# A two-layer graph network on one core: fewer TensorE signals, one-hots behind the visit scans, and a narrower spacing memset in the first layer

## The chip, the cores and the metric

The kernel runs on 1 core of one Trainium2 chip. The metric is device time in microseconds (us) of one execution, as the median of several runs.

## What is computed

`x` holds 3125 nodes of 128 features. There are 53125 directed edges, sorted by their destination node, each with 32 attributes. Two graph layers with 8 heads of 16 features run one after the other, each on the normalised and rectified nodes, and each adds to `x`:

```python
edge_index = jnp.stack([src, dst])
h = jnp.maximum(_layernorm(x, axis=-1), 0.0)
x = x + _L0_gnn_ref(h, L0_gnn_W, L0_gnn_att, L0_gnn_bias, edge_index)
h = jnp.maximum(_layernorm(x, axis=-1), 0.0)
x = x + _L1_gnn_ref(h, edge_index, edge_attr_32, ...)
# layer 0: e = leaky_relu(a_src[src] + a_dst[dst]); softmax over the edges of a dst; sum of alpha * h[src]
# layer 1: score = q[dst].k[src] / 4 + edge_attr @ We + be; softmax over the edges of a dst;
#          sum of attn * v[src]; projection by Wo; + residual; layernorm with gamma, beta
```

## The kernel before

The edges are cut into tiles of 128, and a "visit" is one tile seen by one block of 125 nodes. Sixteen visits make a group, in four quarters of four visits. There are 28 groups; the last one has two quarters, so each layer has 440 visits. In each layer a loop `run_groups` walks over the groups. It is unrolled, and every engine has its own order of work, written out by hand and joined to the others by semaphores. In step g the loop works on three groups at once: group g is scored (`new`), group q = g-1 goes through the running maxima and the exponentials (`mid`), and group r = g-2 is weighted and summed (`old`). There are 30 steps.

GpSimd (POOL) does one thing in the loop: for each visit it issues an indirect DMA that gathers 128 table rows into `G` (L511), and ahead of each it runs `space(300)`, a memset of 300 int32 on one partition (L497) that nothing reads. `G` is a ring of three groups (UNROLL = 3); before each quarter of group g the gathers wait for `pv_ready` of group g-3, which VectorE gives when it has weighted that quarter (`weigh`, L1405). A row is 136 floats in the first layer and 256 in the second.

In the first layer SyncE loads the ids of each group into `lid_ring` (L385, three groups deep) and, every third group, the attributes of three groups into `attr_in` (L404, L407; one buffer). TensorE spreads ids over the partitions (`spread_ids`, L811), and VectorE turns them into transposed one-hots (`node_rows`, L1215, four of them a group, into `ST`). TensorE expands node terms with them (`expand`, L836); VectorE adds the parts (`part_sum`, L1244), then adds the gathered column of all sixteen visits (`score_sum`, L1266, which waits for the gathers of the whole group), and makes the score (`scores`, L1275). TensorE transposes the scores (L870, L871); VectorE scans them (`edge_scans`, L1301, L1302), keeps the last column (`edge_maxima`, L1309); TensorE collects it (L887, semaphore `hop1`); VectorE scans over the visits (`visit_scans`, L1319, L1321, semaphore `x_done`); TensorE spreads the result back (L899, `hop2`). The sums over a group's edges are matmuls in six batches (`sums(g, u, p)`, L851), added into `acc` by VectorE (`add`, L1432); batches 2 to 5 raise `mm_done`. ScalarE makes the one-hots `S` (L615, L619), the exponentials (L655), and copies.

Beside this the first layer prepares the second one's edge bias: TensorE transposes attributes (L932, semaphore `a_T`), ScalarE copies them into `attrT` (L666, `a_Te`), TensorE multiplies them by `WeBD` one step later (L911, semaphore `a_mm`), and ScalarE copies the product (L660, `a_out`). At the start of step 27 VectorE prepares bias rows (`bias_parts`, L1177 to L1186).

In a full step of the first layer TensorE gives 12 semaphore signals: `t_done` twice, `scoreT`, `hop1`, `hop2`, `a_mm`, four of `mm_done`, `a_T` and `al_mm`. VectorE's order around the change is

```python
edge_scans(); rescale(); edge_maxima()
node_rows(2)
visit_scans()
add(0); add(1); carry(); node_rows(3)
```

## Time and profile before

| what | value |
|---|---|
| three runs | 1488.92, 1489.5, 1489.5 us; median 1489.5 us |
| the profiled execution: its own time | 1486.06 us |
| its span, first to last instruction | 1484.3 us |
| mean granted TensorE clock | 0.668 of full speed |
| busy share of PE, DVE, ACT, POOL | 66%, 63%, 43%, 80% |
| gathers of the first layer, first memset to last issue | 37.28 to 688.32 us |
| gathers of the second layer, likewise | 764.04 to 1420.24 us |

The busy share counts an engine's instructions and not its waits. An engine with the highest share need not be the one that sets the end; for that one looks for the engine that never waits for another, and for who waits for it. All times on the axis of the profile are counted from the span's first instruction.

### The profile page before, as it was taken

How to read it: one execution, taken by the hardware profiler on the slowest of the kernel's cores; microseconds unless marked ns; L12 is line 12 of the kernel's file. 1: busy time of each engine (PE TensorE's matmuls, PEld its weight loads, DVE VectorE, ACT ScalarE, POOL GpSimd, SP SyncE). 2: the span in 40 equal slices, each digit the busy share in tenths (PEclk: the TensorE clock that was granted, in tenths of full speed). 3: DMA queues.
4: the chain of work that ended last, by engine and by line, in shares of the span. 5: the costliest groups of instructions: out<-in, count | busy, mean ns of one | idle time of the engine just before them, and what ended most of it. 6: DMA issues, size and time to landing. Idle time of an engine off the chain costs nothing.

```text
span 1484.3 us, 21963 instructions
## 1 busy us (share of the span) xinstructions
PE 980.2 (66%) x4985; PEld 817.4 (55%) x4985; DVE 929.5 (63%) x3002; ACT 636.9 (43%) x1699; POOL 1190.4 (80%) x1806
## 2 busy tenths in 40 slices
PE   5547557777667776676575766676676856566674
PEld 4335446656555565564355655666565746455564
DVE  6446556665665666567834666666666666666578
ACT  5624343453434434341367343444445344444404
POOL 5888888888888888884048888888888888888820
PEclk9655555555555555555686778786867688787765
DMA  6332222222223222222133333333333233333311
GB/s 141 72 69 47 71 49 53 63 71 48 70 48 70 48 69 48 63 48 75 57 112 93 89 88 90 86 89 89 90 89 88 87 89 89 89 89 87 89 29 44
DMA packets 54209, 110.41 MB, mean 74 GB/s; under 512 B 16876, under 2 KB 30848, under 8 KB 53956
## 3 DMA queue, kind: packets, MB, share of 16 engines
q0 software_dynamic: 36288, 91.12, 23.5%
q1 hardware_dynamic: 16483, 17.39, 4.3%
q8 instruction: 46, 0.75, 0.2%
q14 instruction: 79, 0.65, 0.1%
q10 hardware_dynamic: 1313, 0.50, 0.1%
HBM read 100.60 MB, written 8.81 MB: 74 GB/s over the span
## 4 chain that ended last, share of the span: by engine, by line
POOL 39%; issue 6%; DVE 5%; PE 3%; ACT 1%; DMA 0%; DVEq 0%; POOLq 0%; SPq 0%; ACTq 0%
POOL G L511 29%; POOL pad_i L497 10%; PE bank L851 2%; DVE halves L1074 1%; DVE acc L1432 1%; DVE PV L1405 0%; DVE mv L1081 0%; DVE G L1572 0%; DVE hn L1580 0%; DVE xs L1526 0%; DVE hn L1525 0%; DVE hn L1524 0%; PE bank L899 0%; DVE G L1569 0%; DVE hn L1523 0%
## 5 line engine op out<-in xcount | busy, mean ns | idle before, releaser
L511 POOL DMA_INDIRECT G<-table,idx_all x880 | 870.6, 989 | 143.2 <-issue 124.0
L851 PE MATMUL bank<-PV,S 128*125 128x144 f32 x1760 | 446.0, 413 | 135.8 <-DVE PV L1405 74.8
L851 PEld LDWEIGHTS bank<-PV,S 128*125 128x125 f32 x1760 | 369.5, 284 | 164.1 <-issue 121.4
L1432 DVE TENSOR_TENSOR acc<-acc,bank 125x144 f32 x880 | 259.5, 295 | 235.1 <-PE bank L851 154.8
L497 POOL MEMSET pad_i<- 1x300 int32 x880 | 297.1, 338 | 18.8 <-DMA table<-h0b 9.8
L615 ACT ACTIVATE S<-iota_n,lid 128x125 f32<-128x125 f32 x880 | 275.8, 387 | 0.5 <-DVE pen L1169 0.5
L834 PE MATMUL bank<-qe,ST 125*128 x880 | 144.5, 316 | 40.1 <-DVE prod L1225 22.7
L1405 DVE TENSOR_TENSOR PV<-G,PV 128x512 f32<-128x512 f32 x220 | 150.2, 684 | 19.6 <-issue 19.4
L619 ACT ACTIVATE S<-S,ones 128x500 f32<-128x500 f32 x220 | 156.6, 712 | 7.2
L628 ACT ACTIVATE ST<-bank 125x512 f32<-125x512 f32 x110 | 62.6, 596 | 218.7 <-PE bank L899 119.1
L834 PEld LDWEIGHTS bank<-qe,ST 125*128 125x128 f32 x880 | 126.2, 221 | 50.5 <-issue 49.5
L820 PE MATMUL bank<-ident,S 128*125 128x128 f32 x440 | 91.4, 344 | 61.1 <-ACT S L619 50.3
L1225 DVE TENSOR_TENSOR prod<-bank,G 128x512 f32<-128x512 f32 x110 | 74.8, 680 | 87.8 <-DMA G<-table,idx_all 66.9
L820 PEld LDWEIGHTS bank<-ident,S 128*125 128x125 f32 x440 | 79.7, 250 | 67.4 <-ACT S L619 55.6
L655 ACT ACTIVATE EP<-DD 128x256 f32<-128x256 f32 (+1 forms) x56 | 20.2, 360 | 166.6 <-DVE DD L1369 130.8
L1215 DVE TENSOR_SCALAR ST<-bank,vcol 125x512 bf16<-125x512 f32 x110 | 81.5, 743 | 16.2 <-PE bank L811 9.5
L870 PE MATMUL bank<-ident,es 128*128 128x128 f32 x28 | 12.2, 435 | 104.7 <-DVE sc L1275 96.3
L1234 DVE TENSOR_REDUCE raw<-prod 128x32 f32<-128x512 f32 x110 | 74.3, 675 | 1.1
L670 ACT ACTIVATE AL<-bank 125x8 f32<-125x8 f32 x56 | 9.9, 177 | 149.2 <-PE bank L944 125.9
L1266 DVE TENSOR_TENSOR raw<-es,G 128x128 f32<-128x128 f32 x28 | 8.4, 300 | 101.6 <-DMA G<-table,idx_all 99.3
L870 PEld LDWEIGHTS bank<-ident,es 128*128 128x128 f32 x28 | 4.9, 173 | 120.9 <-DVE sc L1275 110.8
L871 PE MATMUL bank<-ident,sc 128*128 128x128 f32 x56 | 23.1, 412 | 68.8 <-DVE sc L1278 64.6
(220 smaller groups left out, 1257.9 us busy)
## 6 DMA issues: line engine op xcount, KB each, us to landing
G<-table,idx_all POOLq DMA_INDIRECT x880
prod<-in_edge_attr_dram SPq DMA_DIRECT2D x8, 672.0 KB
table<-G SPq DMA_DIRECT2D x12, 224.0 KB
bias_rows<-qe SPq DMA_DIRECT2D x1, 1664.0 KB, 5.8
table<-h0b SPq DMA_DIRECT2D x8, 178.5 KB
out_dram<-G SPq DMA_DIRECT2D x8, 168.0 KB
prod<-in_edge_attr_dram SPq DMA_DIRECT2D x8, 90.0 KB
xs<-in_x_dram SPq DMA_DIRECT2D x1, 504.0 KB
```

Of the source, the lines that this page charges most:

```text
L497: pool.memset(pad_flat[0:1, 0:width], 0).then_inc(s_space, 1)
L511: pool.indirect_dma_start(G[:, u, v, 0:w], None, table, bass.IndirectOffsetOnAxis(ap=idx_all[:, g * GV + v:g * GV + v + 1], axis=0)).then_ ...
L615: last = act.activation(S[:, u, v, :], iota_n[:, 0:BN], ACT.Abs, bias=lid[:, bass.ds(g * GV + v, 1)], scale=-1.0)
L619: act.activation(S[:, u, QV * j:QV * j + QV, :], S[:, u, QV * j:QV * j + QV, :], ACT.Relu, bias=ones[:, 0:1], scale=-1.0).then_inc(s.sem[" ...
L820: last = pe.transpose(tp[j % 2][0:BN, k * P:k * P + P], S[:, u, QV * j + k, :], ident[:, :])
L834: last = pe.matmul(ex[j % 2][:, k * F:k * F + F], ST[:, v, :], nodes[:, bass.ds(off, F)], start=True, stop=True)
L851: last = pe.matmul(sums_bank(p)[0:BN, at:at + H * SLOT], S[:, ur, v, :], PV[:, v, :, :].rearrange("p h k -> p (h k)"), start=True, stop=True)
L1215: ve.tensor_scalar(ST_b[:, QV * j:QV * j + QV, :], tp[j % 2][0:BN, :].rearrange("p (v e) -> p v e", v=QV), node, None, op0=ALU.is_equal).t ...
L1225: ve.tensor_tensor(prod[:, j % 2, :].rearrange("p (v f) -> p v f", v=QV), ex[j % 2][:, :].rearrange("p (v f) -> p v f", v=QV), G[:, u, QV ...
L1234: ve.tensor_reduce(raw[:, QV * j:QV * j + QV, :].rearrange("p v h -> p (v h)"), prod[:, j % 2, :].rearrange("p (c d) -> p c d", d=DH), AX. ...
L1405: ve.tensor_tensor(PV[:, QV * j:QV * j + QV, :, 0:DH], rows, PV[:, QV * j:QV * j + QV, :, DH:DH + 1].to_broadcast([P, QV, H, DH]), ALU.mul ...
L1432: ve.tensor_tensor(a, a, o, ALU.add).then_inc(s.sem["acc_added"], 1)
```

## The change

It has three parts, all in the first layer.

1. TensorE gives 9 signals in a full step in place of 12. `t_done` comes after the second `spread_ids` of a group alone (for group 0 also after the fourth); `a_mm` is given for the first group alone, `a_T` for the first two. Who waited for them now waits for a later signal of TensorE that stands behind the same work: the one-hots of the last two quarters and the id loads for `hop1`, the product's readers for batch 2 of the sums (`wait_attr_product`), the transposes' readers for batch 4 (`wait_attr_T`). For that the transposes of the attributes go ahead of batch 4 of the sums in TensorE's order.
2. On VectorE `node_rows(2)` comes behind `visit_scans()`.
3. The spacing memset has 280 columns in the first layer; in the second it keeps 300.

```diff
+        def wait_attr_product(eng, q):
+            if q > 0:
+                wait(eng, L[0]["mm_done"], sums_done(q - 1, 2))
+            else:
+                wait(eng, a_mm, q + 1)
+        def wait_attr_T(eng, g):
+            if g > 1:
+                wait(eng, L[0]["mm_done"], sums_done(g - 2, 4))
+            else:
+                wait(eng, a_T, g + 1)
...
             def load_ids(g, u):
-                wait(sp, L[0]["t_done"], transposed(0, g - UNROLL, 3))
+                wait(sp, L[0]["hop1"], g - UNROLL if g > UNROLL else 0)
+                wait(sp, L[0]["t_done"], 2 if g == UNROLL else 0)
...
-                wait(sp, a_T, g)
+                wait_attr_T(sp, g - 1)
...
-                            space(300)
+                            space(300 if n else 280)
...
-                        wait(act, a_mm, q + 1)
+                        wait_attr_product(act, q)
...
-                            wait(act, a_T, g + 1)
-                            wait(act, a_mm, g)
+                            wait_attr_T(act, g)
+                            wait_attr_product(act, g - 1)
...
-                    if j % 2:
+                    if j == 1 or (j == 3 and g == 0):
                         last.then_inc(s.sem["t_done"], 1)
...
-                        last.then_inc(a_mm, 1)
+                        if q == 0:
+                            last.then_inc(a_mm, 1)
...
-                    if 3 * old > 8:
-                        sums(g, u, 4)
                     if n == 0 and has_attr(g, new):
                         pe.wait_ge(s_attr, 48 * (i + 1))
                         wait(pe, a_Te, g)
                         for k in range(QV):
                             last = pe.transpose(tp[0][:, k * P:k * P + P], attr_in[:, u, k * P:k * P + P], ident[:, :])
-                        last.then_inc(a_T, 1)
+                        if g < 2:
+                            last.then_inc(a_T, 1)
+                    if 3 * old > 8:
+                        sums(g, u, 4)
...
-                wait(ve, a_mm, AG)
+                wait_attr_product(ve, AG - 1)
...
-                        wait(ve, s["t_done"], transposed(0, g, j))
+                        if j < 2 or g == 0:
+                            wait(ve, s["t_done"], g + 1 + (g > 0 or j > 1))
+                        else:
+                            wait(ve, s["hop1"], g)
...
                     edge_maxima()
+                    visit_scans()
                     node_rows(2)
-                    visit_scans()
```

## Rows read from the trace of the kernel before

**Rows 1.** The profile's page: POOL's busy time, and the chain's shares by engine.

```profile
PE 980.2 (66%) x4985; PEld 817.4 (55%) x4985; DVE 929.5 (63%) x3002; ACT 636.9 (43%) x1699; POOL 1190.4 (80%) x1806
...
POOL 39%; issue 6%; DVE 5%; PE 3%; ACT 1%; DMA 0%; DVEq 0%; POOLq 0%; SPq 0%; ACTq 0%
```

**Rows 2.** Waits of POOL, first layer (us in total, times, longest us).

```profile
POOL G L511 <- issue: 63.7, 391, 0.4
POOL pad_i L497 <- DMA table<-h0b: 9.8, 1, 9.8
```

**Rows 3.** Windows of the gathers (L511) alone: first layer, second layer.

```profile
37.28:688.32 651.04, 432.58 (x440) 0.57 0.26 61
...
764.04:1420.24 656.20, 438.05 (x440) 0.75 0.31 89
```

**Rows 4.** Windows of the memsets (L497) alone: first layer.

```profile
37.28:688.32 651.04, 148.56 (x440) 0.57 0.26 61
```

**Rows 5.** Waits of DVE, 76 to 680 us.

```profile
DVE raw L1266 <- DMA G<-table,idx_all: 87.2, 17, 11.5
DVE acc L1432 <- PE bank L851: 83.5, 42, 4.0
DVE acc L1432 <- remote: 26.6, 14, 6.4
```

**Rows 6.** Timeline of POOL, end of group 26 (start us, us, engine, line).

```profile
675.24 0.34 POOL L497 MEMSET pad_i<- 1x300 int32 x1
675.74 0.95 POOL L511 DMA_INDIRECT G<-table,idx_all  x1 [0.16 <-POOL pad_i L497]
```

**Rows 7.** Timeline of DVE, step 26 and what follows.

```profile
673.43 0.55 DVE L1244 TENSOR_REDUCE es<-bank 128x128 f32<-128x384 f32 x1
678.59 0.37 DVE L1266 TENSOR_TENSOR raw<-es,G 128x128 f32<-128x128 f32 x1 [4.61 <-DMA G<-table,idx_all]
...
679.90 0.17 DVE L1177 MEMSET prod<- 96x128 uint32 x1
```

**Rows 8.** Timeline of DVE, steps 27 and 28.

```profile
696.11 0.28 DVE L1266 TENSOR_TENSOR raw<-es,G 128x128 f32<-128x128 f32 x1
...
701.23 0.23 DVE L1319 TENSOR_TENSOR_SCAN D<-rows,D,bank 8x16 f32<-8x16 f32 x1 [0.37 <-PE bank L887]
```

**Rows 9.** Groups by shape: memsets of POOL (busy us, mean ns).

```profile
L497 POOL MEMSET pad_i<- 1x300 int32 x880 | 297.1, 338 | 18.8 <-DMA table<-h0b 9.8 <-DMA table<-G 9.0
...
L453 POOL MEMSET ST<- 112x896 f32 x1 | 0.8, 836 | 0.0
...
L444 POOL MEMSET S<- 8x512 int32 x1 | 0.5, 519 | 0.3 <-POOLq L1607 0.3
...
L447 POOL MEMSET pad_i<- 1x130 int32 x1 | 0.2, 196 | 0.0
```

**Rows 10.** Timeline of POOL between the layers: gathers with no memset between.

```profile
709.33 0.93 POOL L523 DMA_INDIRECT G<-bias_rows,tidx  x1 [0.30 <-issue]
710.56 0.93 POOL L523 DMA_INDIRECT G<-bias_rows,tidx  x1 [0.30 <-issue]
```

**Rows 11.** Timeline of DVE, step 15 around the moved one-hot.

```profile
401.58 0.18 DVE L1309 TENSOR_TENSOR RH<-Vsel,FR 128x32 f32<-128x32 f32 x1
402.31 0.75 DVE L1215 TENSOR_SCALAR ST<-bank,vcol 125x512 bf16<-125x512 f32 x1 [0.55 <-PE bank L811]
402.97 0.23 DVE L1319 TENSOR_TENSOR_SCAN D<-rows,D,bank 8x16 f32<-8x16 f32 x1
```

**Rows 12.** Timeline of PE, the same step.

```profile
402.20 0.28 PE L887 MATMUL bank<-RH,Hsel 128*8 128x32 f32 x2
...
411.61 1.77 PE L851 MATMUL bank<-PV,S 128*125 128x144 f32 x6 [1.16 <-issue]
413.18 1.06 PE L932 MATMUL bank<-ident,prod 128*128 128x128 f32 x4
```

**Rows 13.** Timeline of SyncE's queue: the attributes of groups 15 to 17.

```profile
389.70 0.79 SPq L404 DMA_DIRECT2D prod<-in_edge_attr_dram  x2
```

**Rows 14.** Timeline of POOL and of DVE at one long gather.

```profile
550.94 1.63 POOL L511 DMA_INDIRECT G<-table,idx_all  x1 [0.16 <-POOL pad_i L497]
...
550.87 0.27 DVE L1374 TENSOR_SCALAR OHF<-iota_n,first_lid 8x125 f32<-8x125 f32 x1
```

**Rows 15.** Waits of PE, 76 to 680 us.

```profile
PE bank L870 <- DVE sc L1275: 87.6, 20, 10.8
```

More of the change, by code:

```diff
@@ L266, in gnn_kernel @@
         NODE_SEMS = ("halves", "xc", "std", "inverse", "scales", "hn", "hT_ps", "hT", "feat", "feat_out", "feat_done")
-        LOOP_SEMS = dict(S_ready=QUARTERS, distances=QUARTERS, t_done=2 * GROUPS - 1, st_ready=QUARTERS, expanded=8, qk_done=0,
+        LOOP_SEMS = dict(S_ready=QUARTERS, distances=QUARTERS, t_done=GROUPS + 1, st_ready=QUARTERS, expanded=8, qk_done=0,
                          score_parts=GROUPS, scores_ready=GROUPS, es_ready=GROUPS, scoreT=GROUPS, esT_ready=GROUPS,
```

## The prediction

> **What bounds the kernel now.** I read the page first. GpSimd has the highest busy share, 80%, and the chain that ended last is 39% GpSimd [rows 1]. The chain is drawn back only to 685 us, so its share speaks of the second layer, and the first has to be read from its waits. GpSimd's waits come next. In the first layer's 651.04 us [rows 3] it waits for another engine once, 9.8 us at the start for the table's write; all else is 0.16 us or so between the end of a memset and the gather behind it [rows 2]. It never waits for the ring of three groups. So the stretch is 440 times one period: 651.04 / 440 = 1.480 us, made of a memset of 148.56 / 440 = 0.338 us [rows 4], a gather of 432.58 / 440 = 0.983 us [rows 3], and 0.16 us between them [rows 6]. A group of sixteen takes 23.7 us.
>
> Who waits for GpSimd? VectorE at L1266 stood idle for the gathers 17 times between 76 and 680 us, 87.2 us in all [rows 5], and TensorE behind it 87.6 us for the scores [rows 15]. The last time is in step 26: the last gather of group 26 ends at 675.74 + 0.95 = 676.69 [rows 6], its rows are used at 678.59, 1.9 us later, and VectorE had been idle for 4.61 us [rows 7]. From there the gathers matter no more. Group 27 has only 8 of them, issued by 688.32, and L1266 of that group runs at 696.11 with no wait [rows 8]. So the first layer ends by this path: 432 periods of GpSimd, 1.9 us to land, then steps 26 to 29 at VectorE's and TensorE's own pace (`bias_parts` from 679.90 [rows 7], 696.11 and so on).
>
> **The memset, 300 to 280 columns.** The trace has no memset of 280. Between 130 and 300 columns the time rises from 196 to 338 ns [rows 9], 0.835 ns a column; between 300 and 512 from 338 to 519, 0.854; between 512 and 896 from 519 to 836, 0.826. Twenty columns are 16.5 to 17.1 ns. I take 16.8 ns, near the middle and from the two slopes that meet at 300. On the path lie 432 memsets: 432 x 0.0168 = 7.3 us (bounds 7.1 and 7.4). Does the gather start sooner by as much? From one gather's end to the next's start are now 0.34 + 0.16 = 0.50 us. Gathers with no memset between them follow at 0.30 us and are no longer, 0.93 us [rows 10]. The gap has 0.20 us of room over that, and 0.017 us is far inside it. The lower bound of this term, if the gap grew back in full, would be nothing.
>
> **What gathers cost beside DVE.** A gather is mostly 0.95 us; 440 of them at that would be 418 us, and they took 432.58 [rows 3], so 14.6 us is excess of single long ones. The one at 550.94 took 1.63 us, and on VectorE L1374 (a tensor_scalar from SBUF to SBUF) was running as it began [rows 14]. Such hits hang on where in VectorE's step a gather begins, and a shorter memset shifts that by up to 16 x 0.017 = 0.27 us over a group. The second layer, same memset, has 438.05 / 440 = 0.996 us, 12.4 ns more a gather [rows 3]. If the first layer came to that, 432 x 12.4 ns = 5.4 us would be given back; if it lost as much excess as that, it would gain 5.4 more. I take no change, since VectorE's step stays tied to the gathers by L1266, with 2 us either way. The Trainium skill says why, in its page SBUF — State Buffer, section Who interferes with whom: VectorE in a two-port mode, which a tensor_scalar may enter, and GpSimd lock each other out of a shared pair of ports for a whole instruction. The row at 550.94 agrees with it, and by it the shorter memset would neither add nor remove a hit as such: the sum stays.
>
> **The signals and their new waits.** Three signals fewer on TensorE remove no instruction, only the signal on one. The trace shows no price for a signal alone; below it is nothing, and above it is what TensorE's time could give if it were on the path. It isn't: in the loop VectorE, and TensorE with it, wait for gathers, by 4.61 us in step 26. So I cost it at nothing, in this stretch by that cover. The Trainium skill's page TensorE: Matmul & The Clock Gate, section The cost: per-tile semaphore tail, has 26.3 ns for each signal that ends a matmul; by that three signals in 26 steps would be an estimate of 2.1 us of TensorE's time, and if it lay on the path the sum would be 9.4 us. No row shows it.
>
> The waits that come later: ScalarE's L660 now waits for batch 2 of the sums, and L666 for batch 4 in place of the transposes. Transposes (1.06 us) and batch 4 (1.77 us) change places [rows 12], so that pair ends when it ended. TensorE was even idle for 1.16 us ahead of batch 4, and the transposes need nothing from VectorE, so they go into that gap: up to 1 us of TensorE gained a step, hidden too. Behind batch 4, VectorE's `add(11)` waits, and behind that the step's end; both move inside the cover. SyncE: the attributes of groups 15 to 17 were issued at 389.70 [rows 13] and first used at 413.18, 23.5 us later; the wait comes at most one batch later, 1.77 us. The ids are loaded two steps ahead of their use, and `hop1` comes 0.28 us of matmul behind the last `spread_ids`. Behind these two SyncE's queue holds only the next such loads. Nothing there.
>
> **The one-hot behind the scans.** Now VectorE, done with L1309 at 401.76, idles 0.55 us for the ids, runs the one-hot and finds `hop1` done [rows 11]. After the change it must first wait for L887, which ended at 402.48 [rows 12]: 0.72 us idle in place of 0.55. That is 0.2 us a step; the tail's 0.37 [rows 8], where no one-hot stands there already, is the other reading. The one-hot itself comes some 0.5 us later, and `expand(g, 2)`, `part_sum` and the rest of the score wait for it. All of it has 4.61 us of cover in step 26; without that cover 26 x 0.2 = 5.2 us (9.6 us at 0.37). With the period shorter by 16 x 0.0168 = 0.27 us a group, about 4 us of cover are left. What is late next is still the gathers.
>
> **The tail and the rest.** Step 27 has two quarters, no attributes and no `node_rows(2)`; steps 28 and 29 have no new group. So from 678.59 on the same instructions run, and `bias_parts` waits for batch 2 of step 26 where it waited for the product just ahead of it; VectorE came to it at 679.90 with both long done. The stretch between the layers and the second layer are unchanged: they start 7.3 us sooner. The second layer is tied to its own gathers, 656.20 us [rows 3].
>
> **Sum.** -7.3 us, with nothing for the rest. Against the profiled execution that is 1486.06 - 7.3 = 1478.8 us (its span 1484.3 to 1477.0; 1.8 us lie around the span). The median of the runs is 3.4 us above the profiled execution's time, and I take the difference as it is: 1489.5 - 7.3 = 1482.2 us. 0.2% of the kernel is 3.0 us, which is about what a measurement can tell from no change.
>
> **The rivals.**
> - Collisions eat the gain: gathers get as long on average as in the second layer, 0.996 us. For it: excess varies, and the phase shifts. Against: VectorE's phase follows the gathers. 7.3 - 5.4 = 1.9 us gained, 1487.6 us.
> - Slower by the same hits at full strength: each group has one gather hit as at 550.94, 1.63 - 0.95 = 0.68 us. 27 groups x 0.68 = 18.4 us of excess, on top of the smaller hits the trace now has, against 14.6 now. It decides from the point where a mean gather grows by more than 16.8 ns, so to 1.000 us in the first layer. If all the larger hits came on top of today's excess, it would be +18.4 - 7.3 = 11 us, 1500.6 us. Against: among 440 gathers that have every phase already, most miss. The skill's rule of the lock speaks for the mechanism, not for the number.
> - The loop stops being bound by gathers, because the one-hot's wait and later signals cost more than 4 us a step. Then the first layer grows by the excess over 4 us, 26 times. At 0.2 to 0.4 us of cost it doesn't come to that; what does occur now and then is a long wait of VectorE for TensorE, up to 6.4 us [rows 5]. One of these in step 26 would make L1266 late by 6.4 - 4.3 = 2.1 us: 5.2 us gained, 1484.3 us.
> - The memset doesn't shorten the period (the gap grows back): 1489.5 us. Against it [rows 10].
> - More than forecast: hits get rarer (all of 5.4 us: 12.7 us gained, 1476.8 us), or TensorE's signals count after all (9.4 us, 1480.1 us).
>
> **How the numbers follow.** The forecast, a gain of 5 to 9.5 us with 7.3 as its middle, gets 0.72. It holds the small stall in step 26 and 2 us of hits either way: 1480 to 1484.5 us. More than that gets 0.08. Hits that leave 1 to 3 us get 0.08, no shorter period 0.05, slower by hits 0.05, slower by a loop bound elsewhere 0.02. Faster by over 0.2%: 0.72 + 0.08 = 0.80. Within: 0.13. Slower: 0.07. The range goes from 1478.5 (part of the "more" case) to 1486.0 us (half of the gain of the forecast lost), and leaves about 2 in 10 outside.
>
> **What would show it.** L497 of the first layer at about 321 ns and of the second at 338. The first layer's gathers from 37.3 to about 680.9 us (440 x 16.8 ns = 7.4 sooner), GpSimd with no wait for VectorE. L1266 of group 26 at about 671.3, still waiting for the gathers, by some 4 us. L1319 in mid-layer with a wait of some 0.7 us for L887, and the one-hot with none. L932 ahead of the third last L851 of a step. Between L1266 of group 26 and the end of the span the same 805.7 us as now (1484.3 - 678.59). The prediction is wrong if gathers of the first layer have a mean over 0.99 us, if GpSimd shows waits for L1405, or if L1266 of group 26 no longer waits for them.

## The result and the profile after

| | before | after |
|---|---|---|
| median of 20 runs each, same chip | 1489.5 us (1487.08 to 1491.88) | 1491.41 us (1489.35 to 1494.64) |
| span of the profiled execution | 1484.3 us | 1487.6 us |
| mean granted TensorE clock | 0.668 | 0.687 |

The ratio is 1.0016, with a 95% interval from 1.0009 to 1.0023. The forecast of 1482.2 us was wrong in sign, and its range, 1478.5 to 1486.0 us, doesn't hold the time.

The memset did what was forecast. The windows of the changed kernel's first layer, gathers (L526) in the first line and memsets (L512) in the second (stretch, its length, busy us and count, clock, DMA share, GB/s):

```profile
37.20:693.45 656.25, 444.85 (x440) 0.59 0.25 61
37.20:693.45 656.25, 141.68 (x440) 0.59 0.25 61
```

The memsets take 141.68 / 440 = 322 ns, 16 ns less than in [rows 4], and 6.9 us less in all. The gathers take 444.85 us where they took 432.58 [rows 3]: 1.011 us each, 12.3 us more in all. 12.3 - 6.9 = 5.4 us, and the stretch has grown by 5.2 us, from 651.04 to 656.25. What follows it, from L1286 of group 26 to the end, was 1.9 us shorter (803.8 us against 805.7), so the span grew by 3.3 us. The question of the case is the length of the gathers.

Who waits is as it was, only more so. The changed kernel's waits of POOL, 37 to 694 us, and of DVE, 76 to 690 us (total, times, longest):

```profile
POOL G L526 <- issue: 55.5, 342, 0.4
POOL G L526 <- POOL pad_i L512: 15.8, 98, 0.2
POOL pad_i L512 <- DMA table<-h0b: 9.2, 1, 9.2
...
DVE raw L1286 <- DMA G<-table,idx_all: 162.9, 26, 11.3
DVE acc L1452 <- PE bank L866: 42.1, 30, 1.6
DVE D L1339 <- PE bank L902: 18.5, 25, 0.8
```

GpSimd never waits for VectorE. VectorE waits for gathers in every step, 162.9 us in place of 87.2, and its long waits for TensorE and for "remote" are gone [rows 5]. The wait for `hop1` that the new order makes is there, 18.5 / 25 = 0.74 us a step, and hidden.

Now one full step. The timeline of the changed kernel, POOL and DVE, from 428 to 436 us (start, duration):

```profile
428.71 0.67 DVE L1425 TENSOR_TENSOR PV<-G,PV 128x512 f32<-128x512 f32 x1
428.99 1.23 POOL L526 DMA_INDIRECT G<-table,idx_all  x1 [0.16 <-POOL pad_i L512]
...
432.13 0.95 POOL L526 DMA_INDIRECT G<-table,idx_all  x1 [0.16 <-issue]
433.46 0.27 DVE L1394 TENSOR_SCALAR OHF<-iota_n,first_lid 8x125 f32<-8x125 f32 x1
433.56 1.59 POOL L526 DMA_INDIRECT G<-table,idx_all  x1 [0.16 <-issue]
433.65 0.67 DVE L1425 TENSOR_TENSOR PV<-G,PV 128x512 f32<-128x512 f32 x1
434.47 0.13 DVE L1400 TENSOR_SCALAR DF<-DF 8x1 f32<-8x1 f32 x1
434.96 0.21 DVE L1407 TENSOR_SCALAR R<-ident,DF 8x8 f32<-8x8 f32 x1
```

Two gathers are long here, and a weighting runs in each: `weigh(2)`, of the third quarter, in the first and `weigh(3)` in the second (both L1425). The first weighting ends at 429.38, the gather 0.84 us later, at 430.22; the second ends at 434.32, the gather 0.83 us later. At first I read that the second gather ends with L1407 (435.17), and blamed the streak of small tensor-scalar instructions; the last experiments are about that.

### The profile page after: what moved, and what is told of

It is laid out like the page before. It is cut to its first block, busy times and chain, and to the rows that moved or that the text cites. A ratio compares the mean times of both kernels' runs of the same rounds, so it can differ in the third digit from the quotient of the medians.

```text
span 1487.6 us, 21963 instructions
## 1 busy us (share of the span) xinstructions
PE 919.6 (62%) x4985; PEld 765.0 (51%) x4985; DVE 928.3 (62%) x3002; ACT 637.0 (43%) x1699; POOL 1195.3 (80%) x1806
## 4 chain that ended last, share of the span: by engine, by line
POOL 39%; issue 6%; DVE 5%; PE 3%; ACT 1%; DMA 0%; DVEq 0%; POOLq 0%; SPq 0%; ACTq 0%
POOL G L526 29%; POOL pad_i L512 10%; PE bank L866 2%; DVE halves L1091 1%; DVE acc L1452 1%; DVE PV L1425 0%; DVE mv L1098 0%; DVE G L1592 0%; DVE hn L1600 0%; DVE xs L1546 0%; DVE hn L1545 0%; DVE hn L1544 0%; ACT hn L580 0%; DVE G L1589 0%; DVE hn L1543 0%
## 5 line engine op out<-in xcount | busy, mean ns | idle before, releaser
L526 POOL DMA_INDIRECT G<-table,idx_all x880 | 881.8, 1002 | 142.7 <-issue 110.8
L866 PE MATMUL bank<-PV,S 128*125 128x144 f32 x1760 | 420.3, 395 | 96.6 <-DVE PV L1425 84.0
L866 PEld LDWEIGHTS bank<-PV,S 128*125 128x125 f32 x1760 | 352.1, 271 | 123.6 <-issue 113.8
L1452 DVE TENSOR_TENSOR acc<-acc,bank 125x144 f32 x880 | 259.1, 294 | 122.5 <-PE bank L866 86.4
L512 POOL MEMSET pad_i<- 1x280 int32 (+1 forms) x880 | 290.6, 330 | 17.9 <-DMA table<-h0b 9.2
L1425 DVE TENSOR_TENSOR PV<-G,PV 128x512 f32<-128x512 f32 x220 | 150.3, 684 | 19.3 <-issue 19.2
L849 PE MATMUL bank<-qe,ST 125*128 x880 | 129.6, 293 | 32.4 <-DVE prod L1245 32.2
L849 PEld LDWEIGHTS bank<-qe,ST 125*128 125x128 f32 x880 | 112.5, 200 | 43.1 <-issue 42.3
L1286 DVE TENSOR_TENSOR raw<-es,G 128x128 f32<-128x128 f32 x28 | 8.7, 309 | 174.1 <-DMA G<-table,idx_all 174.1
L835 PE MATMUL bank<-ident,S 128*125 128x128 f32 x440 | 82.1, 317 | 41.8 <-ACT S L634 41.8
L835 PEld LDWEIGHTS bank<-ident,S 128*125 128x125 f32 x440 | 71.1, 226 | 48.1 <-ACT S L634 48.1
L653 ACT ACTIVATE esT<-bank 128x128 f32<-128x128 f32 x28 | 7.8, 278 | 200.8 <-PE bank L886 200.8
L886 PEld LDWEIGHTS bank<-ident,sc 128*128 128x128 f32 x56 | 11.3, 202 | 137.6 <-DVE sc L1298 137.6
L1235 DVE TENSOR_SCALAR ST<-bank,vcol 125x512 bf16<-125x512 f32 x110 | 80.6, 735 | 0.8 <-PE bank L826 0.5
```

Source lines behind the costliest of these rows:

```text
L512: pool.memset(pad_flat[0:1, 0:width], 0).then_inc(s_space, 1)
L526: pool.indirect_dma_start(G[:, u, v, 0:w], None, table, bass.IndirectOffsetOnAxis(ap=idx_all[:, g * GV + v:g * GV + v + 1], axis=0)).then_ ...
L835: last = pe.transpose(tp[j % 2][0:BN, k * P:k * P + P], S[:, u, QV * j + k, :], ident[:, :])
L849: last = pe.matmul(ex[j % 2][:, k * F:k * F + F], ST[:, v, :], nodes[:, bass.ds(off, F)], start=True, stop=True)
L866: last = pe.matmul(sums_bank(p)[0:BN, at:at + H * SLOT], S[:, ur, v, :], PV[:, v, :, :].rearrange("p h k -> p (h k)"), start=True, stop=True)
L1235: ve.tensor_scalar(ST_b[:, QV * j:QV * j + QV, :], tp[j % 2][0:BN, :].rearrange("p (v e) -> p v e", v=QV), node, None, op0=ALU.is_equal).t ...
```

## The experiments

Before in the table is the kernel before, run beside it on the same chip. "Gathers" is the busy time of the first layer's 440. "Held" is worked out from the trace: the excess over 0.951 us of gathers that had a weighting running 0.12 us after their start, or starting later within them. The edits are made to the changed kernel, unless said otherwise. The gathers are those of one profiled execution. For e4 and e12 it was the slowest of all (1509.79 and 1620.08 us), so their columns are left empty; for e2, e3 and e17 too it was the slowest (1501.82, 1537.44 and 1616.79 us), 5 to 12 us above the median.

| run | edit | us | ratio to before | before | gathers | held |
|---|---|---|---|---|---|---|
| e1 | parts 1 and 2, 300 columns | 1491.87 | 1.0032 [1.0017, 1.0046] | 1487.7 | 440.86 | 15.8 |
| e2 | before with 280 | 1496.42 | 1.0058 [1.0036, 1.0080] | 1487.7 | 432.92 | 12.1 |
| e3 | 240 | 1531.24 | 1.0298 [1.0277, 1.0320] | 1487.7 | 425.79 | 4.6 |
| e4 | no tensor_scalar in the streak | 1487.99 | 1.0000 [0.9974, 1.0026] | 1487.7 | - | - |
| e5 | part 1 alone, 300 | 1493.29 | 1.0034 [1.0022, 1.0046] | 1487.1 | 440.10 | 14.2 |
| e6 | part 2 alone, 300 | 1492.64 | 1.0034 [1.0023, 1.0044] | 1487.1 | 440.97 | 14.8 |
| e7 | six more signals a step | 1488.17 | 1.0006 [0.9997, 1.0015] | 1487.1 | 444.13 | 17.6 |
| e8 | none | 1488.11 | 1.0004 [0.9995, 1.0013] | 1487.1 | 444.26 | 22.1 |
| e9 | before, no edit | 1582.52 | 0.9967 [0.9923, 1.0011] | 1586.86 | 435.22 | 12.0 |
| e10 | before with 280 | 1598.94 | 1.0043 [0.9998, 1.0088] | 1586.86 | 426.90 | 5.2 |
| e11 | 240 | 1627.83 | 1.0314 [1.0244, 1.0383] | 1586.86 | 431.26 | 11.8 |
| e12 | as e4 | 1593.06 | 1.0008 [0.9959, 1.0057] | 1586.86 | - | - |
| e13 | before, no edit | 1487.82 | 1.0004 [0.9994, 1.0014] | 1487.24 | 435.26 | 11.0 |
| e14 | before with 280 | 1484.37 | 0.9984 [0.9975, 0.9993] | 1487.24 | 439.87 | 14.8 |
| e15 | 240 | 1473.36 | 0.9904 [0.9889, 0.9919] | 1487.24 | 442.85 | 20.5 |
| e16 | as e4 | 1488.69 | 1.0011 [1.0001, 1.0020] | 1487.24 | 444.50 | 22.4 |
| e17 | `weigh(3)` earlier | 1604.63 | 1.0151 [1.0104, 1.0199] | 1581.42 | 424.11 | 4.7 |
| e18 | 220 | 1643.82 | 1.0398 [1.0343, 1.0453] | 1581.42 | 434.77 | 13.6 |

The table falls in two. In e5 to e8 and e13 to e16 TensorE's signals come on time, and most steps of VectorE have the same form. In the others they come late now and then, by up to 15 us (in e1 hardly: VectorE's waits called "remote" are 2.3 us in all). The chip and the hour have a part in that: one chip gave the kernel before 1487.7 us with e1 to e4 and 1586.86 us with e9 to e12. The kernel has a part too, since beside the 1487.7 us e1 had hardly any late signal and e2 and e3 had many. The two halves answer two questions, and I take them apart.

### Which part costs, and does a narrower memset pay

```diff
-                            space(300 if n else 280)
+                            space(300)
```

> The changed kernel with the memset back at 300 columns, so parts 1 and 2 alone. Theory A (hits by phase): with the signals and the order changed, VectorE's step is regular, each step's OHF instruction comes 13.13 us after L1286, and with a period of 1.450 in place of 1.433 us it begins some 1.16 us after a gather's start, so that the next gather is hit by about 0.47 us in place of 0.64. First-layer gathers: mean 0.998 to 1.008 us (983 ns before, 1011 after). Time: 5 to 10 us over the kernel before, so 1494 to 1499 us, slower than the changed kernel as well. Theory B (the narrower memset itself makes gathers longer): mean 983 ns and the time of the kernel before, within 1 us. Theory C (the later waits cost on the path): L1286 of the first layer waits less for the gathers than the 174 us of the changed kernel.

> The kernel before with the memset of the first layer at 280 columns, so part 3 alone. Theory A (hits by phase): VectorE's step stays irregular, its phases scattered, and the excess over 0.951 us a gather stays near 14 us in the first layer: 7.3 us faster with 3 us either way, 1479 to 1486 us. Theory B (the narrower memset itself makes gathers longer): mean gather near 1.011 us, and the time is that of the kernel before or up to 5 us over it.

> The changed kernel with a memset of 240 columns in the first layer. The period falls by 40 x 0.84 = 34 ns, 432 times 14.5 us. Theory A (hits by phase): ten gathers lie between L1286's landing and OHF, so OHF begins 0.34 us later in the gathers' cycle, about 0.27 us after a gather's start, where the trace of neither kernel has a hit of this kind. The 0.64 us of 26 steps go, 16.6 us; other hits may come up to half of that. Time 1491 - 14.5 - 16.6 = 1460 us, 1458 to 1470 with new hits. Theory B (narrower is longer): the mean gather rises over 1.011 us to 1.04 and more, and little or nothing is gained, 1487 us or over. L1286 still waits for gathers, by some 5 us a step.

e1 lengthened the gathers with no change of the memset. e2 and e3 contradicted the gathers' theory: they got slower although their gathers were hardly longer than in [rows 3], or shorter. The signals explain it. In e3, TensorE's last `hop1` matmul ends at 286.00, and VectorE, which waits for it, goes on at 292.03. The timeline of PE and DVE in e3, and below it its waits of POOL, 76 to 730 us:

```profile
285.72 0.28 PE L902 MATMUL bank<-RH,Hsel 128*8 128x32 f32 x2 [0.46 <-issue]
...
285.48 0.18 DVE L1329 TENSOR_TENSOR RH<-Vsel,FR 128x32 f32<-128x32 f32 x1
292.03 0.24 DVE L1339 TENSOR_TENSOR_SCAN D<-rows,D,bank 8x16 f32<-8x16 f32 x1 [6.37 <-remote]
...
POOL pad_i L512 <- DVE PV L1425: 63.7, 23, 4.8
```

VectorE's step gets longer than the gathers' group, the ring of three groups runs full, and GpSimd waits. Here the gathers no longer set the layer.

### Part 1 alone, part 2 alone, and signals alone

```diff
# e5, against the changed kernel: part 1 without part 2 (and space(300))
                     edge_maxima()
+                    node_rows(2)
                     visit_scans()
-                    node_rows(2)
...
# e6, against the kernel before: part 2
                     edge_maxima()
+                    visit_scans()
                     node_rows(2)
-                    visit_scans()
...
# e7, against the changed kernel: in sums and in expand, first layer
+                    elif n == 0:
+                        last.then_inc(s_extra, 1)
```

> Part 1 alone: 9 signals a step, attribute transposes ahead of batch 4, the one-hot where it was, the memset at 300. Theory A (hits of VectorE's instructions on gathers set the first layer): a regular step, excess of gathers 18 to 24 us against 14, 3 to 8 us slower than before. Theory D (TensorE's signals reach their waiters late, and their number matters): the late signals of the first layer, 208 us summed over those traced before, fall below 50 us, and VectorE waits for L851 and for nothing else of TensorE by less than 60 us against 110. At 300 columns the gathers still set the layer, so D gives the time of before within 3 us.

> Part 2 alone: node_rows(2) behind visit_scans, 12 signals, the memset at 300. Theory A: the step stays as irregular as before, excess 14 us with 3 either way, time of before within 3 us. Theory D: with 12 signals the late ones stay, near 200 us, and the time is that of before within 3 us; if instead the order is what makes TensorE's signals come in time, the late ones fall below 50 us here and not in the run with part 1 alone.

> The changed kernel (280 columns) with six more signals a step of the first layer, raised by TensorE on a semaphore that nobody waits for: after batches 0 and 1 of the sums and after each of the four expands. Nothing else differs. Theory D (the number of signals makes TensorE's signals late): late ones come back, GpSimd waits for L1425, and the time is that of the memset alone or over it, 1496 us and more. Theory A: extra signals change nothing but the phase, within 3 us of the changed kernel run beside it.

> The changed kernel itself, beside the others on the same chip. Theory A and D both expect 0.1 to 0.3% over the kernel before. Its profile: if its 0 late signals of the first profile are a property of the kernel, they are 0 again; if they come and go from run to run, this one will show some, and a first layer that ends otherwise.

Each part alone, with 300 columns, costs 0.34%, and their gathers are 4.8 and 5.7 us longer than e13's, which ran on another chip. The costs don't add: with both parts (e1) it is 0.32%, and 5.6 us. Six signals more a step don't change the time: 1488.17 beside 1488.11 us. They do move the hits: `weigh(2)` and `weigh(3)` account for 17 us of excess in e7 and for 21 in e8, and other instructions for the rest of nearly the same sum (25.7 and 25.8 us), which is in part luck. So the count of signals has no price that can be measured here, and e6, with all 12, has no late ones either.

### The disturbed chip once more

> The kernel before itself, for a profile of an execution in which TensorE's signals come in time. Theory A (hits of VectorE's instructions on gathers): VectorE's step is regular, and the excess of the first layer's gathers is smaller than the 22 us that part 1 and part 2 gave alone at 300 columns, by the 5 us that these cost: 16 to 18 us. Theory E (the gain and loss lie in late signals, and in an execution without them all versions at 300 are alike): excess 22 us as with part 1 or part 2.

> The kernel before with 280 columns, once more. Theory A alone, in an execution without late signals: 7.3 us less for the period, and the excess moves with the phase: ten gathers later OHF comes 0.17 us later in the cycle, up to 0.17 us more for each hit in 26 steps, so up to 4.4 us given back for each kind of hit: 1480 to 1487 us. Theory F (a denser stream of gathers brings TensorE's late signals on): late signals again, GpSimd waits for L1405, 1491 us and more, on this chip as on the first.

> The changed kernel with 240 columns, once more. Theory A alone: 14.5 us less for the period and the largest hit gone, 1460 to 1470 us, VectorE still waits for gathers by 4 us a step. Theory F (denser gathers bring late signals on): late signals in nearly every step of the first layer, GpSimd waits for L1425 over 30 us, 1525 us and more again, whatever the chip.

> The changed kernel with OHF, DF and R as instructions with two tensor inputs in the first layer, for a profile of an ordinary execution: the first one profiled was one of its slowest (1509.79 us against a median of 1487.99). Theory A in the narrow form (the three tensor_scalars hold gathers up): no long gather ends with R any more, first-layer excess 26 us down to some 11, and 10 to 15 us faster than the changed kernel. If the streak of instructions from L1425 on does it as a whole, the long gathers still end with R, excess stays at 22 us or over, and the time is that of the changed kernel within 3 us, as the medians of the first call suggest.

The waits of DVE in e9, the kernel before itself, 76 to 680 us:

```profile
DVE acc L1432 <- remote: 88.6, 38, 8.3
DVE acc L1432 <- PE bank L851: 71.1, 34, 4.2
...
DVE raw L1266 <- DMA G<-table,idx_all: 17.3, 2, 11.7
```

VectorE waits for gathers 2 times where it should 26 times. So in this state TensorE's late signals set the layer, also in the kernel before, and a shorter memset has nothing to give. Of the 84.6 us that e9's span has over e13's, only 17.0 had come up by the last gather of the first layer (707.38 against 690.38 us); the rest comes behind it. 240 columns cost 3% again, on the same chip as in e3. Why narrower is worse, and not merely the same, is open. Theory F, that denser gathers bring the late signals, fits the numbers of e3, e11 and e18. As e11's expectation puts it, "whatever the chip", it falls with e14 and e15 below: the same kernels, on another chip, had no late signal. At most it holds on a chip that is disposed to them.

### The same with signals on time

```diff
# e4, e12 and e16, first layer (L1400 likewise, as a scalar_tensor_tensor)
-ve.tensor_scalar(OHF[:, :], iota_n[0:H, 0:BN], first_lid[:, bass.ds(q, 1)], None, op0=ALU.is_equal)
+ve.tensor_tensor(OHF[:, :], iota_n[0:H, 0:BN], first_lid[:, bass.ds(q, 1)].to_broadcast([H, BN]), ALU.is_equal)
...
-ve.tensor_scalar(R8[:, :], ident[0:H, 0:H], DF[:, 1:2], None, op0=ALU.mult)
+ve.tensor_tensor(R8[:, :], ident[0:H, 0:H], DF[:, 1:2].to_broadcast([H, H]), ALU.mult)
```

> The changed kernel, but in the first layer the three tensor_scalar instructions from SBUF to SBUF (OHF, DF, R) are given as instructions with two tensor inputs that compute the same values. Theory A in its narrow form (a tensor_scalar from SBUF to SBUF holds the gather up until it ends): the 25 long gathers that end with R go, 15 us of excess, mean gather 0.977 us, time 1476 us, with 3 us for phases. If the hit comes from L1425 or from the adds between, or if any VectorE instruction with SBUF inputs does it, the mean stays near 1.011 us and the time at 1491 us.

> The kernel before, for a profile of a calm execution (none of TensorE's signals late). Theory A (hits): regular step, first-layer excess 16 to 18 us, 5 us less than with part 1 or part 2 alone (22 us). If the chip is not calm, late signals over 200 us in sum, and the run tells nothing on A.

> The kernel before with 280 columns in a calm execution. Theory A: 7.3 us less for the period, up to 4.4 us back from each kind of hit: 0.1 to 0.5% faster than the kernel before, late signals none. Theory F (a denser stream of gathers brings late signals on by itself): late signals and GpSimd waiting for L1405 though the kernel before shows none on the same chip; 0.2% slower or more.

> The changed kernel with 240 columns in a calm execution. Theory A: 14.5 us less for the period and the largest hit gone, some 1.5 to 2% faster than the kernel before. Theory F: late signals though the kernel before has none, and slower by 2 to 3%, as on the two chips where this ratio was 1.030 and 1.031.

> The changed kernel with OHF, DF and R as instructions with two tensor inputs, in a calm execution. Theory A in the narrow form: no long gather ends with R, first-layer excess 26 us down to some 11, 0.7 to 1% faster than the changed kernel, so 0.6 to 1% faster than the kernel before. If the streak of VectorE instructions holds gathers up as a whole: excess still 22 us or over, and the ratio to the kernel before 1.000 to 1.002.

With 280 columns alone the memsets are 6.9 us shorter, and 4.6 us come back as longer gathers (435.26 to 439.87); the kernel is 0.16% faster. (The expectation of e15 speaks of two chips with 1.030 and 1.031; it was one chip at two times.) All three parts together bring the gathers to 444.26 us (e8), and nothing is left. With 240 columns the gain is 1%, since the memsets give 22.0 us and the gathers take 7.6.

The same place of the step in e13 and in e16, timelines of POOL and DVE:

```profile
431.45 0.34 DVE L1374 TENSOR_SCALAR OHF<-iota_n,first_lid 8x125 f32<-8x125 f32 x1
431.88 1.27 POOL L511 DMA_INDIRECT G<-table,idx_all  x1 [0.16 <-issue]
431.64 0.67 DVE L1405 TENSOR_TENSOR PV<-G,PV 128x512 f32<-128x512 f32 x1
```

```profile
145.97 1.59 POOL L526 DMA_INDIRECT G<-table,idx_all  x1 [0.16 <-issue]
...
145.86 0.27 DVE L1395 TENSOR_TENSOR OHF<-iota_n,first_lid 8x125 f32<-8x125 f32 x1
146.06 0.67 DVE L1434 TENSOR_TENSOR PV<-G,PV 128x512 f32<-128x512 f32 x1
```

In e13 the gather starts 0.43 us after the comparison and is 0.32 us too long; in the changed kernel it starts 0.10 us after it (0.11 in e16) and is 0.64 us too long. In both it ends 0.83 to 0.84 us after the weighting (432.31 and 433.15 in e13). So the hit is larger by the shift of the phase, and since VectorE's step is tied to the gathers, most steps have the same one: of the 25 steps, 21 of the changed kernel start that gather at 0.10 to 0.12 us, and 17 of e13 at 0.42 or 0.43.

That is half of the story. The other half is `weigh(2)`, the first weighting of the changed kernel's timeline above. In e13 most of them start late in a gather and are over before the next:

```profile
426.09 0.95 POOL L511 DMA_INDIRECT G<-table,idx_all  x1 [0.16 <-issue]
...
426.70 0.67 DVE L1405 TENSOR_TENSOR PV<-G,PV 128x512 f32<-128x512 f32 x1
```

This one starts 0.61 us into the gather, which stays at 0.95 us. In the changed kernel a gather starts 0.28 us after it and takes 1.23 us. Summed over the layer, gathers that met `weigh(2)` had 1.0 us of excess in e13 and 6.3 in e8, those that met `weigh(3)` 9.1 and 14.9, all others 6.8 and 4.6. No part alone brings `weigh(2)` to this: it is 1.9 us in e5, 2.3 in e6 and 1.9 in e14, 3.8 in e1 and 6.4 in the changed kernel's first profile.

With the comparison and the scaling as tensor_tensor (e16) the hit stays. My theory of the tensor-scalar forms fell there.

### What in VectorE's streak holds the gather

```diff
                     node_maxima()
+                    if n == 0:
+                        weigh(3)
                     add(6)
                     differences()
-                    weigh(3)
+                    if n:
+                        weigh(3)
```

> The changed kernel, but in the first layer the weighting of the last quarter (L1425 in the changed kernel) stands ahead of the seventh addition, in VectorE's wait for TensorE, and no longer between the comparison L1394 and the difference L1400. Theory A1, the weighting is the instruction in the streak L1394 to L1407 that holds a gather: the 25 gathers of 1.59 us that end with L1407 (15 us over 0.951 us in the changed kernel) are gone, the excess of the first layer falls from 25.8 us to 11 to 16 us, and the time to 1473 to 1479 us (ratio to the changed kernel's 1.0004: 0.990 to 0.995). Theory A2, any back-to-back streak of VectorE holds it, whatever is in it: the streak is 0.67 us shorter, so the hit falls from 0.60 to some 0.2 us a step, or moves to the end of the weighting, and the excess stays within 4 us of 26 if it does that; time 1484 to 1490 us. Rival F, late TensorE signals (only on a chip that shows them): the time is that of the changed kernel within 0.3%, as the move shortens no wait for TensorE.

> The changed kernel with 220 columns in the first layer. Theory A, the gathers set the layer and VectorE's phase adds to them: the memset falls from 322 to some 271 ns (240 columns took 288 ns), 440 x 51 ns = 22 us less than 280 columns. If the next gather then starts ahead of L1394 in every step, as it did in a third of the steps with 240 columns, the 15 us of gathers held to L1407 go as well: 1450 to 1458 us. If it doesn't, 1463 to 1470 us. Theory F, denser gathers bring late signals of TensorE on a chip that has them: GpSimd waits for L1425 30 times or more, and the time is above 1.02 of the kernel before on the same chip. Theory G, a second bound shows (GpSimd waits for the ring although no signal is late, since a step of TensorE and VectorE takes no less than some 22 us): waits of POOL for L1425, and 1470 us or more.

Both fell on a chip with late signals, so their times don't answer what was asked, and no version faster than e15 came of them. Their traces do answer. The timeline of e17, POOL and DVE, first at the old place of `weigh(3)`, then at `weigh(0)` and `weigh(1)` of the step:

```profile
431.95 0.96 POOL L526 DMA_INDIRECT G<-table,idx_all  x1 [0.16 <-issue]
...
431.82 0.27 DVE L1394 TENSOR_SCALAR OHF<-iota_n,first_lid 8x125 f32<-8x125 f32 x1
...
589.72 0.95 POOL L526 DMA_INDIRECT G<-table,idx_all  x1 [0.16 <-issue]
...
589.53 0.27 DVE L1394 TENSOR_SCALAR OHF<-iota_n,first_lid 8x125 f32<-8x125 f32 x1
...
362.00 1.44 POOL L526 DMA_INDIRECT G<-table,idx_all  x1 [0.16 <-issue]
363.92 1.30 POOL L526 DMA_INDIRECT G<-table,idx_all  x1 [0.16 <-issue]
...
361.92 0.69 DVE L1425 TENSOR_TENSOR PV<-G,PV 128x512 f32<-128x512 f32 x1 [0.20 <-issue]
363.71 0.68 DVE L1425 TENSOR_TENSOR PV<-G,PV 128x512 f32<-128x512 f32 x1
```

The gather at 431.95 starts 0.13 us after the comparison, nearly the phase of the changed kernel's large hit, and the one at 589.72 starts 0.19 us after it. In the changed kernel they would be some 0.61 and 0.55 us too long, counted from the 0.64 us at 0.10; with the weighting gone from there they take 0.96 and 0.95 us, and so do the others that start 0.2 to 0.7 us after a comparison (330.96, 351.99). They are few, since late signals scatter the phases. Beside the weightings at 361.92 and 363.71 gathers are long, and end 0.83 us after them (362.61 and 363.44; 364.39 and 365.22). And in e18, at one step where L1407 comes late:

```profile
145.67 1.47 POOL L526 DMA_INDIRECT G<-table,idx_all  x1 [0.16 <-issue]
...
145.64 0.67 DVE L1425 TENSOR_TENSOR PV<-G,PV 128x512 f32<-128x512 f32 x1
...
147.69 0.30 DVE L1452 TENSOR_TENSOR acc<-acc,bank 125x144 f32 x1 [1.10 <-remote]
147.91 0.21 DVE L1407 TENSOR_SCALAR R<-ident,DF 8x8 f32<-8x8 f32 x1
```

The gather ends at 147.14, before L1407 has begun, and again 0.83 us after the weighting (146.31). So it is the weighting, theory A1. A gather whose start plus 0.12 us falls into a weighting ends 0.83 us after it. That holds within 40 ns for 48 of 48 such gathers of the changed kernel, 34 of 34 in e13, 39 of 39 in e14 and 52 of 52 in e16, but for 51 of 52 in e8, 29 of 36 in e15, 25 of 34 in e3 and 34 of 39 in e9, with one to three exceptions in five more traces. All of them take 0.95 us, and in all the weighting began about when the gather did or within 0.12 us after it. Where it had begun 0.05 us or more before the gather, the rule holds 533 times in 533 over all twenty traces.

The Trainium skill has the rule behind it, in SBUF — State Buffer, section Who interferes with whom: a VectorE instruction with two inputs in SBUF contends with a GpSimd instruction that reads SBUF. The trace agrees, as L1425 has both inputs (G and PV) there and the gather reads its ids (`idx_all`) from there. L1286, whose inputs `es` and `G` are both in SBUF, does the same: over all twenty traces, 235 of 235 gathers that began 0.05 us or more behind it, with it still running 0.12 us in, end 0.83 us after it, and counted likewise no gather was long under instructions with an input in PSUM (0 of 375 under L1264, 0 of 1003 under L1235, 0 of 445 under the additions L1452, or their lines in the other kernels). The same section infers that such a tensor_tensor leaves the making of descriptors alone; here it lengthens a gather by 0.64 us in most steps, and the measurement decides. That the read of the ids is what waits was not tried.

## Why the prediction was wrong

- **Bound: right.** Gathers set the first layer. L1286 of group 26 starts at 683.80, having waited 6.21 us for the last of them (it ended at 681.90); after it 803.8 us follow to the end, where 805.7 were forecast.
- **Memset: right.** 16 ns each against 16.8. The gap behind it stayed at 0.16 us.
- **Length of the gathers: the step that failed.** "I take no change, since VectorE's step stays tied to the gathers by L1266, with 2 us either way." The tie works the other way round. It gives most steps the same phase, so a shift of a few tenths of a microsecond changes the same hit in some 20 of 25 steps and little averages out. Measured: +12.3 us against the traced execution of before, +9.0 us (435.26 to 444.26) against one whose signals were on time. The held part went from 11.0 to 22.1 us, about half of it by each of `weigh(2)` and `weigh(3)`, and the rest of the excess fell by 2 us. The trace of before has 14.1 us of excess over 0.951 us (14.6 over the prediction's 0.95) against 16.9 in e13. Late signals had scattered its phases: among its gathers the one behind L1374 starts anywhere from 0 to 1.3 us after it, and once 2.2.
- **The rival that came true** is the one given 0.05: hits at full strength. It was worked out with one hit of 0.68 us a group on top. It is one of 0.64 us in most groups, but it replaces one of 0.32, and a second one of some 0.28 that was not there; so the sign turned by little. Its turning point, a mean of 1.000 us, was passed (1.011).
- **Why those 0.68 us: wrong instruction.** The prediction named the comparison L1374 at the long gather [rows 14], as the tensor_scalar that was running at its start, and leant on the rule of the two-port mode. The comparison was over at 551.14, and a lock for its length leaves 0.2 us of wait and not 0.68. The weighting behind it, L1405, holds the gather, by the other rule in that section of the Trainium skill, of two SBUF inputs. The row shown was one line short of that. In the kernel before it ends at 551.73, and the gather 0.84 us later, at 552.57:

```profile
551.06 0.67 DVE L1405 TENSOR_TENSOR PV<-G,PV 128x512 f32<-128x512 f32 x1
```

- **Number of signals: right.** It has no price of its own (e7 beside e8). The prediction's other estimate, 2.1 us for three signals a step by the Trainium skill's TensorE: Matmul & The Clock Gate, section The cost: per-tile semaphore tail, is not borne out on a path that gathers set. Part 1 as a whole did cost, by the phase, as the next point says.
- **The moved one-hot: right in price, wrong in its cover.** The wait for L902 is 0.74 us, against 0.72 forecast, and hidden. But a hidden delay still moves VectorE's phase; part 2 alone made gathers 5.7 us longer (e6), part 1 alone 4.8 us (e5), each against e13. Costing both at nothing because of 4.61 us of cover was the same error as above.
- **Shown and not shown.** Shown: the weighting as holder (e13, e16, e17, e18), what each part does alone (e5, e6, e14, with e8; the three sum to 15.1 us of gathers where all together cost 9.0), no price for the number of signals (e7). Not shown: where late signals come from, and why a narrower memset loses 3% beside them. Profiled executions with late signals also had the lower granted clocks (0.639 to 0.673 against 0.659 to 0.710); which of the two brings the other was not tried. That the change ended at 1.0016 on one chip and 1.0004 on another is left open; the intervals overlap.

## What to carry to other kernels

Where an engine on the path is lengthened by another engine's instruction, that is a price by phase and not by count: find the instruction (line its ends up with the ends of the long ones), and cost each reordering as a shift of that phase, repeated in most steps, even if the delay itself is hidden. A profile with late signals hides such a pattern; one with signals on time shows it. And look at every instruction of the kind that holds: here half of the loss came from a second weighting, which missed all but a few gathers before the change. A spacing that pays 1% on one chip (240 columns, 0.9904) can cost 3% on another (1.0298, 1.0314), so it wants both measured.

## What the runs showed of the hardware

- A gather by indirect DMA on GpSimd takes 0.951 us alone. If VectorE began to multiply two SBUF operands of 128 x 512 at least 0.05 us before the gather and is still at it when the gather is 0.12 us old, the gather ends 0.83 us after that instruction (533 of 533).
- Where the multiplication begins later, from 0.05 us before to 0.28 us after the gather's start, it depends on what VectorE ran just ahead of it. Behind the comparison L1394 (as tensor_scalar or as tensor_tensor) 192 of 194 such gathers were held in full; behind an addition L1452 30 of 54; behind the one-hot L1235, the maximum L1309 or the scan L1380 none of 156. The changed kernel's large hit is of this kind: its weighting begins 0.09 us into the gather. In e15 the gather starts just ahead of the comparison in 17 steps and the weighting comes 0.2 us in; 16 of them are 0.75 us too long. So the comparison has a part in it, although alone it holds nothing (431.95 in e17). What that part is stays open. So is what the scans do: of 289 gathers that began under L1380, whose inputs are all in SBUF, 109 were long, and 27 ended 0.83 us after it.
- TensorE's signals can reach VectorE 6 us late (286.00 to 292.03 in e3) and up to 15 us (in e11 the `hop1` matmul ends at 102.69 and VectorE goes on at 117.66). One chip ran the kernel before in 1487.7 us at one time and in 1586.86 us half an hour later, and its granted clock was 0.648 in e9, where e13 on another chip had 0.683.
